# Attention and feed-forward in one kernel: value products in two parts of 256 query columns, half jobs placed by a build-time table, and one chunk more ahead of the loop

## What is computed

```python
q, k, v = (split_heads(xn @ W + b) for W, b in ((Wq, bq), (Wk, bk), (Wv, bv)))      # 16 heads of 8
scores = einsum('bhqd,bhkd->bhqk', q, k) / sqrt(8) + slope[h] * (k_pos - k_pos.T)    # a bias by head
attn = softmax(scores, axis=-1)
att = einsum('bhqk,bhkd->bhqd', attn, v).reshape(B, S, E) @ Wo + bo
# fq: blocks of 16 along the last axis, scaled by max|x|/6 and rounded to the FP4 grid
h = silu(fq(xn) @ fq(w_gate).T) * (fq(xn) @ fq(w_up).T)                              # 352 columns
out = x + att + fq(h) @ fq(w_down).T
```

## Time and profile before

| | |
|---|---|
| median of 3 runs | 901.21 us (895.38 to 918.01) |
| the profiled execution | 894.07 us |
| its span, first to last instruction | 892.3 us |
| TensorE busy (PE) | 772.9 us, 87% |
| VectorE busy (DVE) | 741.1 us, 83% |
| ScalarE busy (ACT) | 633.0 us, 71% |
| GpSimd busy (POOL) | 349.3 us, 39% |
| mean granted TensorE clock | 0.962 |

### The profile page before, as it was taken

One profiled execution on the slowest core, in us unless ns is written; L12 is line 12 of the kernel. 1 busy time (PEld: TensorE's weight loads), 2 busy tenths in 40 slices (PEclk: granted clock), 3 DMA queues, 4 the chain that ended last, 5 costly groups with the idle time before them and its releaser, 6 DMA issues.

```text
span 892.3 us, 13552 instructions
## 1 busy us (share of the span) xinstructions
PE 772.9 (87%) x4939; PEld 225.7 (25%) x4939; DVE 741.1 (83%) x878; ACT 633.0 (71%) x1262; POOL 349.3 (39%) x271
## 2 busy tenths in 40 slices
PE   3279989898989989897989989898989898979896
PEld 2012223221223323231323323222213231313222
DVE  7898898889888888978898888989897989898920
ACT  4106878777777878776877778777777687767775
POOL 7272172624226373715053553615152505141320
PEclk9557999999999999999999999999999999999999
DMA  5900020131001020320102020310102000000000
GB/s 156 256 13 2 1 72 3 52 92 36 3 13 37 13 72 2 101 44 1 37 2 49 13 73 1 107 37 1 37 2 49 13 3 1 2 1 2 2 1 24
DMA packets 32826, 31.83 MB, mean 36 GB/s; under 512 B 4344, under 2 KB 26552, under 8 KB 32760
## 3 DMA queue, kind: packets, MB, share of 16 engines
q1 hardware_dynamic: 32760, 30.96, 12.8%
HBM read 15.91 MB, written 15.04 MB: 35 GB/s over the span
## 4 chain that ended last, share of the span: by engine, by line
PE 58%; DVE 27%; ACT 8%; issue 4%; POOL 2%; DMA 1%; SPq 0%; ACTq 0%; DVEq 0%; POOLq 0%
PE low L966 22%; DVE neg_max L811 19%; PE mx L936 18%; ACT probs L630 6%; PE low L955 5%; PE mx L1005 3%; PE mx L989 3%; PE low L983 2%; DVE am L784 1%; DVE mb L804 1%; PE low L922 1%; ACT pv_s L667 1%; PE low L997 1%; DVE hid L826 1%; DVE inv L798 1%
## 5 line engine op out<-in xcount | busy, mean ns | idle before, releaser
L811 DVE TENSOR_REDUCE neg_max<-mx 128x1 f32<-128x1024 f32 x512 | 611.6, 1221 | 91.6 <-PE mx L936 80.2
L630 ACT ACTIVATE probs<-low 128x512 f32<-128x512 f32 x1024 | 552.0, 603 | 182.1 <-PE low L955 180.4
L936 PE MATMUL mx<-k_op,q_op 51*128 51x512 bf16 x1024 | 318.5, 398 | 55.9 <-DVE neg_max L811 33.4
L955 PE MATMUL low<-q_op,k_op 53*128 53x512 bf16 x1024 | 329.0, 389 | 8.0 <-ACT probs L630 2.5
L966 PE MATMUL low<-probs,v_op 128*32 128x512 f32 x2048 | 277.4, 614 | 7.1 <-ACT pv_s L667 5.9
L551 POOL TENSOR_SCALAR tanh_s<-tanh_s 128x704 f32<-128x704 f32 x16 | 31.7, 1982 | 313.7 <-ACT gate_s L681 313.7
L936 PEld LDWEIGHTS mx<-k_op,q_op 51*128 51x128 bf16 x1024 | 62.6, 95 | 358.5 <-DVE neg_max L811 197.2
L955 PEld LDWEIGHTS low<-q_op,k_op 53*128 53x128 bf16 x1024 | 68.5, 94 | 76.5 <-ACT probs L630 63.8
L489 POOL TENSOR_SCALAR mb<-mb 128x960 f32<-128x960 f32 (+2 forms) x17 | 58.8, 3456 | 39.6 <-DVE mb L804 37.9
L966 PEld LDWEIGHTS low<-probs,v_op 128*32 128x32 f32 x2048 | 40.5, 108 | 89.9 <-issue 46.1
L477 POOL TENSOR_TENSOR zb<-hid,inv 128x704 f32<-128x704 f32 x16 | 22.2, 1387 | 97.7 <-DVEq L799 97.7
(11 more groups left out here) (120 smaller groups left out, 522.3 us busy)
## 6 DMA issues: line engine op xcount, KB each, us to landing
q_op<-q_rows SPq DMA_DIRECT2D x32, 192.0 KB, 3.8
k_op<-k_rows SPq DMA_DIRECT2D x32, 192.0 KB, 4.7
q_rows<-qp SPq DMA_DIRECT2D x8, 384.0 KB, 2.6
k_rows<-kp SPq DMA_DIRECT2D x8, 384.0 KB, 3.2
x_s<-in_L_attn_inputs_dram SPq DMA_DIRECT2D x8, 256.0 KB, 3.7
q_rows<-qp SPq DMA_DIRECT2D x8, 256.0 KB, 3.1
k_rows<-kp SPq DMA_DIRECT2D x8, 256.0 KB, 3.1
out_dram<-o_s SPq DMA_DIRECT2D x8, 256.0 KB, 2.3
```

The lines of the kernel that those rows point to most:

```text
L630: nc.scalar.activation(probs[U % 3][:, 2 * g + x, :], bank("exp", U, j), ACT.Exp).then_inc(st_free, 1)
L811: nc.vector.tensor_reduce(to, slot("max", pos)[:], AX.X, ALU.max, negate=True).then_inc(mx_free, 1)
L936: ins = nc.tensor.matmul(slot("max", pos)[:, 512 * kh:512 * kh + 512], q, k, start=True, stop=True)
L955: nc.tensor.matmul(bank("exp", U, j), k_op[quad][r, g, kt * P:(kt + 1) * P], q_op[quad][r, g, half * HALF:(half + 1) * HALF], start=True, ...
```

## The change

- LEAD goes from 22 to 23: one chunk more before the loop, and every chunk of the loop is one position further on. `HEAD` and `chunk` stay as they are.
- The value product of unit U - 1 is cut into two parts of 256 query columns. Part 0 stands after part 0 of the unit (before the middle jobs), part 1 after part 1. For kt = 0 part 0 is left out and part 1 has all 512 columns.
- `up`, `down` and `wo` become two jobs each, of one token tile (`wo`: two), each with a ring place and a slot of its own, on TensorE and VectorE.
- A table `AT` built by `plan()` gives every job its unit; no unit has two jobs of the same place. Jobs in MIDDLE stay between part 0 and part 1; all others stand at the unit's end, on TensorE, ScalarE and VectorE. The feed-forward part begins at unit 4.
- ScalarE copies `pv` after exponential 0 of its unit. Block maxima follow the second half of `up` at once, the scales a unit later, and the inverses one chunk behind the scales. GpSimd normalizes both groups of a batch in one unit (1, 61, 121) and makes the parts of q and k in one (`parts_unit`). SP follows the table.

```diff
-LEAD = 22
+LEAD = 23
+FFN_FIRST, FFN_STEP = 4, 15
+MIDDLE = ("gate", "q", "k", "v", "gT", "uT", "dT", "bvo")
+def plan():
+    at, busy = {}, set()
+    def put(first, *job):
+        place = job[0] in MIDDLE
+        while (first, place) in busy:
+            first += 1
+        busy.add((first, place))
+        at[job] = first
+        return first
+    for U, job in enumerate(("bvo", "gT", "uT", "dT")):
+        put(U, job)
+    for m in range(HALVES):
+        if m >= LEAD // 16:
+            put(turn_unit(m), "turn", m)
+        put(KT * (m + 1) + 2, "pvT", m)
+    x_at = put(FFN_FIRST, "xT", 0)
+    for p in range(NP):
+        U = put(x_at + 1, "gate", p, 0)
+        U = put(U + 1, "gate", p, 1)
+        U = put(U + 2, "up", p, 0)
+        up = put(U + 1, "up", p, 1)
+        if p + 1 < NP:
+            x_at = put(max(FFN_FIRST + FFN_STEP * (p + 1), up + 7), "xT", p + 1)
+        U = put(up + 7, "hT", p, 0)
+        U = put(U + 1, "hT", p, 1)
+        U = put(U + 1, "down", p, 0)
+        put(U + 1, "down", p, 1)
...
-            def value_product(U):
+            def value_product(U, part):
                 b, quad, half, kt = unit_of(U)
+                if kt == 0 and part == 0:
+                    return
+                cols = slice(0 if kt == 0 else part * HALF // 2, (part + 1) * HALF // 2)
...
-                    ins = nc.tensor.matmul(pv[32 * hh:32 * hh + 32, :], v_op[b % 2][:, kt, 4 * quad + hh, :],
-                                           probs[U % 3][:, hh, :], start=(kt == 0), stop=(kt == KT - 1),
+                    ins = nc.tensor.matmul(pv[32 * hh:32 * hh + 32, cols], v_op[b % 2][:, kt, 4 * quad + hh, :],
+                                           probs[U % 3][:, hh, cols], start=(kt == 0), stop=(kt == KT - 1 and part == 1),
                                            tile_position=(0, 32 * hh))
-                ins.then_inc(pv_done, 1)
+                if part == 1:
+                    ins.then_inc(pv_done, 1)
...
                 elif kind == "up":
-                    free_slot("up", p)
+                    t = job[2]
+                    free_slot("up", p, t)
                     pe.wait_ge(st_free, max(ST["xT", p], ST["uT",]) + 1)
-                    for t in range(2):
-                        ins = nc.tensor.matmul(slot("up", p)[:, 512 * t:512 * t + I], xqT[:, t * P:(t + 1) * P], uT_s[:],
-                                               start=True, stop=True)
-                    ins.then_inc(mx_full, 1)
+                    nc.tensor.matmul(slot("up", p, t)[:, 0:I], xqT[:, t * P:(t + 1) * P], uT_s[:],
+                                     start=True, stop=True).then_inc(mx_full, 1)
...
-            for U in range(NU + KT):
+            for U in range(NU + 2 * KT):
                 for i in range(2):
                     pos = LEAD + 2 * U + i
                     for kh in range(2):
...
                             half_chunk(pos, kh)
                         if U < NU:
                             score(U, 2 * i + kh)
-                    for job in extras(U) if i == 0 else ():
+                    if 0 < U <= NU:
+                        value_product(U - 1, i)
+                    for job in middle(U) if i == 0 else ():
                         job_on_array(job)
-                if 0 < U <= NU:
-                    value_product(U - 1)
+                for job in end(U):
+                    job_on_array(job)
```

More of the change, by code:

```diff
@@ L101 @@
 HEAD = ((1, 0), (1, 1), (0, 0), (0, 1))
[L104 to L121, removed]
@@ L124, with norm_unit, parts_unit @@
-IN_DVE_RING = ("up", "down", "pvT", "wo", "bvo")
+def norm_unit(b):
+    return 1 if b == 1 else 60 * b - 59
+def parts_unit(g):
+    return 60 * (g // 2 - 1) + 16 + 15 * (g % 2)
+def plan():
[25 more added lines that the diff above has]
+        put(U + 1, "down", p, 1)
+    for b in range(1, B):
+        for g in (2 * b, 2 * b + 1):
+            U = norm_unit(b) + 1 + 8 * (g % 2)
+            for name in ("xnT", "q", "k"):
+                U = put(U + 1, name, g)
+            assert U < parts_unit(g)
+            put(max(U, QUADS * UNITS * (b - 1) + 2) + 1, "v", g)
+    for hb in range(2 * B):
+        U = put(at["pvT", hb // 2 * 8 + 6 + hb % 2] + 1, "ctxT", hb)
+        for i in range(2):
+            U = put(max(U, at["down", 2 * hb + 1, 1]) + 1, "wo", hb, i)
+    return at
@@ L127, in rings, with middle, end @@
+AT = plan()
+JOBS = {}
+for _job, _unit in AT.items():
+    JOBS.setdefault(_unit, []).append(_job)
+def middle(U):
+    return [job for job in JOBS.get(U, ()) if job[0] in MIDDLE]
+def end(U):
+    return [job for job in JOBS.get(U, ()) if job[0] not in MIDDLE]
 def rings():
@@ L401, in _ @@
             max_rows(0)
[L402 to L405, removed]
+            for U in range(NU + 2 * KT):
+                for job in JOBS.get(U - 1, ()):
+                    if job[0] == "turn":
+                        max_rows(job[1])
                 for g in range(2, NG):
-                    if group_unit(g) + 8 == U:
+                    if parts_unit(g) + 4 == U:
                         parts_to_dram(g)
@@ L655, in _ @@
             keep_turn(0)
-            for U in range(NU + KT):
+            for U in range(NU + 2 * KT):
                 if 3 <= U < NU:
                     act.wait_ge(pv_done, U - 2)
-                for j in range(2):
+                for j in range(4):
                     exponential(U, j)
[L662 to L711, removed]
@@ new lines, in _ @@
+                    if j == 0 and U % KT == 1 and KT < U <= NU + 1:
+                        m = U // KT - 1
+                        act.wait_ge(pv_done, U - 1)
+                        if m:
+                            act.wait_ge(mx_full, MX["pvT", m - 1] + 1)
+                        nc.scalar.copy(pv_s[:], pv).then_inc(pv_kept, 1)
+                    for job in middle(U) if j == 1 else ():
+                        job_on_scalar(job)
+                for job in end(U):
+                    job_on_scalar(job)
@@ L872, in _ @@
             block_scales(0)
+            block_inverses(0)
             for pos in range(LEAD):
@@ L1000, in job_on_array @@
                 elif kind == "down":
-                    free_slot("down", p)
-                    pe.wait_ge(st_free, max(ST["hT", p, 1], ST["dT",]) + 1)
-                    for t in range(2):
-                        for c, (_, n) in enumerate(IC):
-                            ins = nc.tensor.matmul(slot("down", p)[:, t * P:(t + 1) * P], hqT[t][0:n, c * P:(c + 1) * P],
-                                                   dT_s[0:n, c * P:(c + 1) * P], start=(c == 0), stop=(c == 2))
+                    t = job[2]
+                    free_slot("down", p, t)
+                    pe.wait_ge(st_free, max(ST["hT", p, t], ST["dT",]) + 1)
+                    for c, (_, n) in enumerate(IC):
+                        ins = nc.tensor.matmul(slot("down", p, t)[:, 0:P], hqT[t][0:n, c * P:(c + 1) * P],
+                                               dT_s[0:n, c * P:(c + 1) * P], start=(c == 0), stop=(c == 2))
                     ins.then_inc(mx_full, 1)
```

145 lines of the change are left out of this document (98 added, 47 removed).

## The result

The changed kernel takes 1084.25 us (four runs, 1080.91 to 1085.36) where the kernel before takes 898.3; the ratio is 1.2096, 95% interval 1.203 to 1.2161. The direction and the cause of most of it were forecast, the size was not: 1038 us was predicted and 1075 was the end of the range.

What follows compares the result with a forecast made beforehand. VectorE was taken to bound the kernel before, TensorE the changed one: 67.9 to loop start + 941 work + 4 clock + 10 stalls + 8.4 tail = 1031 us span, 1033 execution, 1038 median; range 985 to 1075.

Steps and rivals of the forecast that it cites:

- What bounds the kernel before, and its room: Loop of the kernel before: VectorE is the fuller engine, TensorE has 674 us of work in 817, 143 spare.
- The parity and its price: LEAD 23 puts each loop chunk on its scores' partition half, so they run serially, 0.22 us each: 207 us added.
- Value parts: Value products cut in two: 331 us of TensorE against 279, +52; even chunk spacing makes VectorE wait less.
- The sum of TensorE's work: Loop of the changed kernel: 433 + 331 + 177 = 941 us, over the 817 there are, so TensorE becomes the bound.
- One sign: Expected in the new profile: TensorE's waits for VectorE shrink under 40 us.
- The clock: Low clock at the loop's start slows some 2 units by 2 us each: +4 us.
- The upper end: High end of the range: stalls 40 us instead of 10 and the median's 7, given as 1075 us.
- Rival 1: Chains of four same-half matmuls: third and fourth wait 0.09 us for weight loads, 88 us more, about 1125 us; chance 0.06.
- Rival 4: TensorE's strict order: VectorE and ScalarE bursts cost 0.25 us a unit instead of 0.04, +54, about 1090 us; chance 0.07.
- The table: New job order: TensorE's waits for turn inputs go, GpSimd's 19 us a round fits seven units; costed at nothing.
- Lead and head: Before the loop: one chunk more costs 1.2 us on VectorE, so the loop starts at 67.9 us instead of 66.7.

Runs made afterwards that it cites:

- e1_pairs: Changed kernel with HEAD turned round, so each chunk again lies on the other partition half from its scores; 902.81 us, ratio 1.0035.
- e6_split_only: Kernel before with only the value product cut in two parts, at the places of the changed kernel; 891.72 us, ratio 0.9923.
- e3_double: Changed kernel with HEAD turned round and every half chunk and score issued twice, always a pair on two partition halves; 1047.87 us, ratio 1.1655.
- e8_cols256: Changed kernel with every half chunk and score cut into two matmuls of 256 columns, all on one partition half; 1068.04 to 1136.68 us, middle 1097.53.
- e4_whole: Changed kernel with the value product whole again after part 1, chunks and scores still on one half; 1009.54 to 1044.94 us, middle 1039.91.
- e9_lead22: Changed kernel with LEAD back at 22 and HEAD as it is; 896.74 us, ratio 0.9966.
- e10_lead22_order: Changed kernel with the edits of e9_lead22 and of e11_order together; 885.56 us, ratio 0.9841.
- e2_lead_only: Kernel before with LEAD 23 and nothing else; 1053.59 us in the middle of four runs from 1025.47 to 1059.79.
- e7_rows64: Changed kernel with score matmuls reading 64 partitions instead of 53; two runs 1055.9 us, others 1120 and 1195 us.
- e11_order: Changed kernel with GpSimd's last normalization moved from unit 121 to 120 and group 7's q and k parts from 151 to 155; 1068.9 to 1183.7 us.

## Why the prediction was right and wrong

- **What bounds the kernel before, and its room.** Right in kind: with the pairs restored, 60 us more of TensorE's work cost 0.35% (e1_pairs), so there was room.
- **The parity and its price.** Right. Chunk and score start 0.22 us apart, and LEAD 23 alone takes the kernel before to 1054 us.
- **Value parts.** Their price of TensorE was right: 0.57 us and an entry of 0.09. Their worth to VectorE was right in kind; e6_split_only puts it at 0.8%.
- **The sum of TensorE's work.** Right: 941 us of work and 10 of stalls are 3.71 us a unit; measured 3.66 at full clock. One sign did not come: TensorE's wait for VectorE before chunks was to fall under 40 us and is 106.8. It is a wait of the weight loads, which run one matmul ahead; the matmuls themselves wait 11.5 us there, and the full-clock units are no longer than the count.
- **The clock: the term that failed.** "Some 2 units x 2: +4" covered the end of the head and nothing after. I had taken the clock of the kernel before, 0.98 in the loop, for granted, because TensorE would only be busier. Measured between the first score and 1075 us: 141 us at half clock. Of each us at half clock, 1 - 3.66 / 6.55 = 0.44 is lost, so 62 us where the term had 4. The balance: 70.9 to the first score, 256 x 3.66 = 937, 62, and 8.5 of tail are 1078 of the 1083.5 us of span; the wait of 5.2 us at 543, which lies in no full-clock unit, is about the rest. e3_double ties the long spells to the half-empty array: with the same spacing of starts and both halves in use, 17 us at half clock after 70 us. e8_cols256 excludes the count of matmuls, e4_whole the value parts.
  The warning stood in the earlier trace rows, and I read it wrongly: TensorE was not "mostly waiting" from 50 to 75 us but busy for 20.18 of the 25 us, at half clock all the while. Ahead of the first score at 66.7 it made chunks, with no score on the other half beside them, and the records of two chunks cover 2.17 of 2.35 us from start to start:

```profile
52.73 2.17 PE L936 MATMUL mx<-k_op,q_op 51*128 51x512 bf16 x4 [0.19 <-DVE neg_max L811]
55.08 2.16 PE L936 MATMUL mx<-k_op,q_op 51*128 51x512 bf16 x4 [0.18 <-DVE neg_max L811]
```

  The clock rose at 77.6 us, after the pairs had begun. By itself that proves nothing, but it is a low clock beside a busy TensorE that fills one half at a time, and the change brings such a stream into the loop.
- **The upper end.** By its own terms it is 1033 - 10 + 40 + 7 = 1070, not 1075; either way the measured time is outside.
- **Rival 1, weight loads in the open.** Did not come. The loads of the changed kernel at 510 us:

```profile
510.06 0.09 PEld L990 LDWEIGHTS mx<-k_op,q_op 51*128 51x128 bf16 x1 [0.41 <-issue]
510.08 0.10 PEld L1009 LDWEIGHTS low<-q_op,k_op 53*128 53x128 bf16 x1
510.29 0.10 PEld L990 LDWEIGHTS mx<-k_op,q_op 51*128 51x128 bf16 x1
510.51 0.09 PEld L1009 LDWEIGHTS low<-q_op,k_op 53*128 53x128 bf16 x1
```

  Each load starts with the matmul ahead of its own (the third matmul starts at 510.51, its load at 510.29) and is done before its turn. The Trainium skill (TensorE: Matmul & The Clock Gate, Part 3, "The mechanism") says in its list of what overlaps that loads overlap running matmuls only where the row group differs; its first paragraph also lets a load for the background weight buffer run ahead. Here the row group is the same in a chain of four and the loads overlap, so the narrower sentence does not hold, and the measurement decides; whether that buffer is the reason, no run here shows.
- **Rival 4, queues lock.** Its time, 1090 us, is near the measured one, but its mechanism did not come: TensorE's waits are in the full-clock units, and these are faster than forecast.
- **The table costs nothing.** Wrong, though small. I had held GpSimd's mean load against seven units and not looked at what lies in its queue ahead of a normalization. Mending two such places gained 11 us (e9_lead22 against e10_lead22_order), 7.3 of them the waits themselves.
- **Lead and head.** The first score was at 70.9 us, not 67.9; the head's wait for the first keys was 18.2 us instead of 14.4. e4_whole, which does the same work ahead of the loop, has its first score at 67.2 us, so this differs from run to run. Nor did the changed kernel's median lie above its profiled run (1084 and 1085), as I had assumed with 5 us.

What stays open: what starts and ends a low spell. In the changed kernel one began in a wait of 5 us, one after a wait of 1.3 and one after 0.6, and in these kernels they lasted from 3 to 314 us. Only their being long in kernels that fill one half at a time is shown: with chunks and scores in pairs, low spells of the loop lasted 3.4 to 10 us. The single longer one of these kernels, 17 us from 850 in e6_split_only, lies where no chunks are left and the scores are again alone on one half.

## What to carry to other kernels

When two streams of small matmuls share the array by partition halves, write down for each step which half each is on before you move one by a position: a constant that looks like a prologue length can hold the parity. Then count the bound engine's work from start to start, and put the clock into the forecast as a term with its own range, not as a constant taken from the kernel before. When a table places jobs for several engines, read each engine's own queue at the places where two jobs meet.

## What the runs showed of the hardware

- Matmuls of 512 bf16 columns on two partition halves start together, on one half 0.22 us apart, each with weights of its own, and their loads of 0.09 to 0.10 us stay hidden in chains of four (e1_pairs at 585 us, the changed kernel at 510 us).
- A busy TensorE is not enough to get the 2.4 GHz level back: in the changed kernel it stayed away for 61 us (from 682.5), in e11_order for 314, with TensorE busy nearly all the time. With chunks and scores on one half, single runs were granted 0.815 to 0.942 on average (e2_lead_only, e4_whole, e7_rows64, e8_cols256, e11_order and the changed kernel); with the same starts on both halves 0.971 in each of four runs. The averages of other paired kernels reach down to 0.928 (the kernel before, in runs of 915 to 920 us that left no trace), so the average alone does not tell the two kinds apart. In the traces of the loops the length of the spells does.
- Such a kernel's time is not one number. The runs of e11_order go from 1069 to 1184 us. Its half-clock time in two of them follows from span and mean clock, 2 x 1181.8 x 0.18 = 425 us and 2 x 1067 x 0.077 = 164 us; the 261 us between them at 0.44 are 115 us, an estimate, and the two runs, 1183.7 and 1068.9, are 114.8 apart.
